# First FFN's down product: two classes as half-array pairs, against four classes as 32-row strips with the weights as the stationary operand

## The reference, cut to what matters

```python
x = x + down(silu(gate(c)) * up(c))     # first FFN, c = per-batch 64x64 condition matrix times x (64 x 64 x 512)
                                        # gate, up: 2048 x 512, down: 512 x 2048, each a cubic spline (Catmull-Rom)
                                        # through 8134 control points laid along the flattened matrix
y = x @ W.T + scale[a] * (x @ A[a].T) @ B[a].T    # adapted layer, a = adapter of the batch (8, rank 16)
x = x + top-2-of-8 experts(y)                     # F = 352, softmax over the two
```

## Time and profile before

| | us |
|---|---|
| runs (median of 3; lowest, highest) | 1277.27; 1273.51, 1279.76 |
| span of the profiled execution (the page gives no other time of it) | 1274.5 |
| PE busy in the span | 1161.4 (91%) |
| PEld / DVE / ACT / POOL busy | 1073.4 / 647.9 / 476.7 / 679.1 |

### The profile page before, as it was taken

The page is one execution under the profiler, slowest core; times in us unless marked ns, Lnnn a source line. Parts: engine busy times, 40 slices in busy tenths (PEclk is TensorE's granted clock), DMA queues, the critical chain, the costliest instruction groups (busy, mean ns, idle before and its releaser), DMA issues. The chain is left out here.

```text
span 1274.5 us, 29820 instructions
## 1 busy us (share of the span) xinstructions
PE 1161.4 (91%) x9814; PEld 1073.4 (84%) x9815; DVE 647.9 (51%) x1223; ACT 476.7 (37%) x1023; POOL 679.1 (53%) x1035
## 2 busy tenths in 40 slices
...
PEclk9769999999999999997999967999999999999998
...
DMA packets 75085, 187.07 MB, mean 147 GB/s; under 512 B 12992, under 2 KB 26056, under 8 KB 70704
## 3 DMA queue, kind: packets, MB, share of 16 engines
...
## 5 line engine op out<-in xcount | busy, mean ns | idle before, releaser
L880 POOL TENSOR_TENSOR in_lo<-inner,in_hi 128x512 fp32r<-128x512 f32 x128 | 168.6, 1317 | 133.4 <-ACT in_hi L1034 133.2
L1577 POOL TENSOR_TENSOR idle<-small 128x1 f32<-128x1 f32 x284 | 93.3, 331 | 196.7 <-DMA out<-result,scatter_at 123.9
L1655 PE MATMUL banks<-slots,zt_hi 128*128 x568 | 190.4, 335 | 4.9 <-DVE zt_lo L1744 2.9
L1657 PE MATMUL banks<-slots,zt_lo 128*128 x568 | 183.8, 324 | 0.0
L1656 PE MATMUL banks<-slots,zt_hi 128*128 x568 | 183.3, 323 | 0.0
L957 PE MATMUL banks<-down_hi,in_hi 64*128 64x320 f32 x1024 | 164.9, 308 | 0.0
L957 PE MATMUL banks<-down_lo,in_hi 64*128 64x320 f32 x1024 | 164.9, 307 | 0.0
L957 PE MATMUL banks<-down_hi,in_lo 64*128 64x320 f32 x1024 | 164.5, 307 | 0.0
L1756 DVE TENSOR_TENSOR hid<-silu_g,banks 128x352 f32<-128x352 f32 x71 | 37.0, 521 | 208.7 <-PE banks L1657 208.7
L1600 POOL DMA_INDIRECT out<-result,scatter_at x71 | 113.7, 1601 | 26.4 <-issue 22.7
L874 POOL TENSOR_TENSOR f_lo<-f_sum,f_hi 128x256 fp32r<-128x256 f32 x128 | 96.3, 769 | 37.8 <-ACT f_hi L1025 34.7
...
## 6 DMA issues: line engine op xcount, KB each, us to landing
...
```

The lines of the kernel that those rows point to most:

```text
L880: nc.gpsimd.tensor_tensor(in_lo[:, cs, :], inner[u % 2][:, :, :], in_hi[:, cs, :].bitcast(F32), ALU.subtract).then_inc(in_done, 1)
L1577: nc.gpsimd.tensor_tensor(idle[:, at:at + 1], small[:, 0:1], small[:, 0:1], ALU.add)
L1655: nc.tensor.matmul(psum[bank][:, 0:FD], zt_hi[:, k, :], w_high, start=(k == 0), stop=False)
L1657: ins = nc.tensor.matmul(psum[bank][:, 0:FD], zt_lo[:, k, :], w_high, start=False, stop=(k == DK - 1))
```

## The change

- **Classes.** The 2048 inner rows and 512 outputs are sorted into 4 classes instead of 2 (32 rows of every chunk and 128 outputs each). A few rows that fall in another class than their output are put right by constants (`c_fix`).
- **Down.** The weights are stationary and the tokens move: 256 columns for both subtiles at once. The four classes take rows 0 to 31, 32 to 63, 64 to 95 and 96 to 127 of the array, each into a bank of its own: three products for a class's outputs (columns 0 to 255 of its bank), two for its powers (columns 256 to 511). All 16 chunks run in two batches of four u, in v = 7 and in v = 1 of the next tile.
- **Sums.** The output is transposed already, so `turn` goes. ACT copies the sums of classes 0 and 3, DVE adds up those of the inner ones (`add_sums`), three steps are split, and `across` has 18 matmuls. One `add` of 1024 elements per tile; x1 is stored transposed, once a tile, into `x1t_dram`.
- **Features.** The condition matrices lie as they are, no longer block-diagonal: each batch's 64 rows make one of a half-array pair. Two groups are one batch (i), i = 3 of a tile comes in v = 0 of its own tile; there are two misc banks, filled and drained together. Moments of both subtiles stand in v = 2.
- **Expert parts.** The three of the down weights come first, and POOL takes their low halves.
- **Layer.** x1 comes transposed into one buffer (two half loads); high and low halves are taken from it directly. PE transposes it back for `out`, ACT copies that (`token_rows`), SP stores it. Expert loads are issued after these, each waiting for the one before.
- **Host side.** Inputs are laid out to fit (tokens of a subtile taken from batches two apart, the residual transposed).
- **Preparation.** The coefficient products are made in two halves (6 matmuls of 256 columns per chunk instead of 3 of 512), with a few small DVE operations for the fix.

The core of the diff (the common indentation is cut):

```diff
-TURN, CLASSES, DPIECES, DWIN = 128, 2, 16, 20
-CLASS_I, CLASS_D = INTER // CLASSES, D // CLASSES
+TURN, CLASSES, DPIECES, DWIN = 89, 4, 16, 20
+CLASS_I, CLASS_D, ROWS = INTER // CLASSES, D // CLASSES, P // CLASSES
+STEPS, STRAYS = CLASSES - 1, 2
...
+def load_x1(sp, t):
+    for h in range(LTILE // TILE):
+        sp.dma_start(x1[:, :, h * TILE:(h + 1) * TILE], x1t_dram[bass.ds(LTILE // TILE * t + h, 1)].rearrange("a p (k n) -> p (a k) n", k=DK)).then_inc(x1_loaded, 16)
...
+PARTS = FC + DK
+DOWN_AT = {1: [(-1, 4), (-1, 5), (-1, 6), (-1, 7)], 7: [(0, 0), (0, 1), (0, 2), (0, 3)]}
+MOMENTS_AT, SUMS_AT, ACROSS_AT, ADD_AT = 2, 2, 3, 4
+FEATURES_AT = {0: [(0, 3)], 4: [(1, 0)], 5: [(1, 1)], 6: [(1, 2)]}
+HIGH_FEATURES_AT = {1: [(0, 3)], 5: [(1, 0)], 6: [(1, 1)], 7: [(1, 2)]}
+PART_AT = {3: [0], 4: [1], 5: [2, 3], 6: [4, 5], 7: [6]}
+F_USES = PAIRS // 2
+USES = 1 + F_USES
...
+def features(t, i):
+    if i == 0:
+        pe.wait_ge(pair_done, t + 1)
+    pe.wait_ge(misc_drained, USES * t + i + 1)
+    for g in (2 * i, 2 * i + 1):
+        at = g % 2 * TILE
         for s in range(SUB):
+            for w, feat in enumerate((feat_hi, feat_lo)):
+                for h in range(2):
+                    rows = slice(h * SEQ, (h + 1) * SEQ)
+                    to = view(misc_bank[h], at + s * SEQ, [[P, 2 - w], [1, SEQ]])
+                    ins = nc.tensor.matmul(to, feat[rows, s, 2 * g:2 * g + 2, :].rearrange("p a n -> p (a n)"), pair[rows, s, 0:2 - w, :],
+                                           start=(w == 0), stop=(w == 1))
+    ins.then_inc(feat_filled, 1)
...
-def down(t, s, u):
+def down(t, u):
     pe.wait_ge(in_done, PAIRS * t + u + 1)
     if u == 0 and not is_int(t, 0):
-        pe.wait_ge(added[s], t)
+        pe.wait_ge(res_added, t)
     for c in (2 * u, 2 * u + 1):
-        for i, (x, w) in enumerate(((in_hi, down_hi), (in_hi, down_lo), (in_lo, down_hi))):
-            for j in range(CLASSES):
-                rows = slice(j * NF, (j + 1) * NF)
-                ins = nc.tensor.matmul(out_bank[s][:, j, 0:NF + CLASS_D], x[rows, c, s * P:(s + 1) * P], w[rows, c, :],
-                                       start=(c == 0 and i == 0), stop=(c == IC - 1 and i == 2))
+        for i, (w, x) in enumerate(((down_hi, in_hi), (down_lo, in_hi), (down_hi, in_lo), (mom_w, in_hi), (mom_w, in_lo))):
+            cols = slice(0, TILE) if i < 3 else slice(TILE, 2 * TILE)
+            for r in range(CLASSES):
+                rows = slice(r * ROWS, (r + 1) * ROWS)
+                ins = nc.tensor.matmul(out_bank[r][:, cols], w[rows, c, :], x[rows, c, :],
+                                       start=(c == 0 and i == 0), stop=(c == IC - 1 and i in (2, 4)), skip_group_check=True)
     if u == PAIRS - 1:
-        ins.then_inc(direct_done[s], 1)
...
+        ins.then_inc(direct_done, 1)
+def across(t):
+    for step in range(STEPS):
+        pe.wait_ge(sums_low, STEPS * t + step + 1)
+        for side, k in ((0, step + 1), (1, STEPS - 1 - step)):
+            item = k - 1 if side == 0 else STEPS + k
+            for i, (w, x) in enumerate(((across_hi, sums_hi), (across_lo, sums_hi), (across_hi, sums_lo))):
+                ins = nc.tensor.matmul(out_bank[k][:, 0:TILE], w[:, item, :], x[:, step, side, :],
+                                       start=False, stop=(i == 2), skip_group_check=True)
+    ins.then_inc(sum_done, 1)
 def body(t):
     for v in range(PAIRS):
         if has_own(t):
             gate_up(t, v)
-        for s, dt, u in DOWN_AT[v]:
-            if has_own(t) if dt == 0 else has_last(t):
-                down(t + dt, s, u)
-        if has_last(t) and v in ACROSS_AT:
-            across(t, t - 1, ACROSS_AT[v])
-        if has_next(t) and v in MOMENTS_AT:
-            moments(t, t + 1, MOMENTS_AT[v])
-        if has_last(t) and v in TURN_AT:
-            turn(t, t - 1, TURN_AT[v])
-        if has_next(t):
-            for g in FEATURES_AT.get(v, []):
-                features(t, t + 1, g)
+        for dt, i in FEATURES_AT.get(v, []):
+            if has(t, dt):
+                features(t + dt, i)
+        for dt, u in DOWN_AT.get(v, []):
+            if has(t, dt):
+                down(t + dt, u)
+        if v == MOMENTS_AT and has_next(t):
+            moments(t + 1)
+        if v == ACROSS_AT and has_last(t):
+            across(t - 1)
...
-def copy_sums(t, s):
-    act.wait_ge(direct_done[s], t + 1)
-    nc.scalar.activation(sums_tok[:, :, :], out_bank[s][:, :, 0:NF], ACT.Copy).then_inc(sums_copied, 1)
-def high_sums(at, s):
-    bank, use = misc_use(at, f"t{s}")
-    act.wait_ge(misc_filled[bank], use + 1)
-    nc.scalar.activation(sums_hi[:, :], misc_bank[bank][:, 0:P], ACT.Copy).then_inc(sums_high, 1)
+def copy_sums(t):
+    act.wait_ge(direct_done, t + 1)
+    nc.scalar.activation(sums[:, 0, :, :], psum[:, OUT:OUT + CLASSES:CLASSES - 1, TILE:], ACT.Copy).then_inc(sums_copied, 1)
+def high_sums(t, step):
+    if step == 0:
+        act.wait_ge(sums_copied, t + 1)
+    else:
+        act.wait_ge(sums_added, (STEPS - 1) * t + step)
+    nc.scalar.activation(sums_hi[:, step, :, :], sums[:, step, :, :], ACT.Copy).then_inc(sums_high, 1)
...
+if v == SUMS_AT and has_last(t):
+    copy_sums(t - 1)
+    high_sums(t - 1, 0)
+if v == MOMENTS_AT + 1 and has_next(t):
+    high_moments(t + 1, 0)
 if has_own(t):
     gate(t, v)
-if v == 0 and has_own(t) and not is_int(t, 0):
-    high_feature(t - 1, PAIRS - 1)
-if has_next(t):
-    for g in FEATURES_AT.get(v - 1, []):
-        high_feature(t, g)
+for dt, i in HIGH_FEATURES_AT.get(v, []):
+    if has(t, dt):
+        high_feature(t + dt, 2 * i)
+        high_feature(t + dt, 2 * i + 1)
+if v == SUMS_AT and has_last(t):
+    high_sums(t - 1, 1)
+    high_sums(t - 1, 2)
+if v == MOMENTS_AT + 1 and has_next(t):
+    high_moments(t + 1, 1)
 if has_own(t):
     high_inner(t, v)
-if has_next(t) and v == 0:
-    pairs(t + 1)
-if has_next(t) and v < SUB:
+if v < SUB and has_next(t):
+    if v == 0:
+        pairs(t + 1)
     high_raw(t + 1, v)
-if has_last(t) and v in COPY_AT:
-    copy_sums(t - 1, COPY_AT[v])
-if has_next(t) and v in MOMENTS_AT:
-    high_moments(t, MOMENTS_AT[v])
-if has_last(t) and v in TURN_AT:
-    high_sums(t, TURN_AT[v])
...
+def add_sums(t, step):
+    if step == 1:
+        dve.wait_ge(sums_copied, t + 1)
+        nc.vector.tensor_tensor(sums[:, 1, :, :], sums[:, 0, :, :], psum[:, OUT + 1:OUT + 3, TILE:], ALU.add).then_inc(sums_added, 1)
+        return
+    dve.wait_ge(sums_added, (STEPS - 1) * t + 1)
+    for side in range(2):
+        ins = nc.vector.tensor_tensor(sums[:, 2, side, :], sums[:, 1, side, :], out_bank[2 - side][:, TILE:], ALU.add)
+    ins.then_inc(sums_added, 1)
+def low_sums(t, step):
+    dve.wait_ge(sums_high, STEPS * t + step + 1)
+    nc.vector.tensor_tensor(sums_lo[:, step, :, :], sums[:, step, :, :], sums_hi[:, step, :, :].bitcast(F32), ALU.subtract).then_inc(sums_low, 1)
+def add(t):
+    dve.wait_ge(res_loaded, 16 * (t + 1))
+    dve.wait_ge(sum_done, t + 1)
+    nc.vector.tensor_tensor(x_res, psum[:, OUT:OUT + CLASSES, 0:TILE], x_res, ALU.add).then_inc(res_added, 1)
...
 for v in range(PAIRS):
+    if v == SUMS_AT and has_last(t):
+        add_sums(t - 1, 1)
+        add_sums(t - 1, 2)
+    if v == MOMENTS_AT + 1 and has_next(t):
+        low_moments(t + 1, 0)
+    if v == ADD_AT and has_last(t):
+        add(t - 1)
     if has_own(t):
         multiply(t, v)
+    if v == MOMENTS_AT + 1 and has_next(t):
+        low_moments(t + 1, 1)
+    if v == SUMS_AT and has_last(t):
+        for step in range(STEPS):
+            low_sums(t - 1, step)
+    for dt, i in FEATURES_AT.get(v, []):
+        if has(t, dt):
+            sum_features(t + dt, i)
+    if v == 0 and has_next(t):
         pairs(t + 1)
+    if v == 1 and has_next(t):
+        for s in range(SUB):
+            low_raw(t + 1, s)
     if has_own(t):
         for i in PART_AT.get(v, []):
...
+def store_out(t):
+    sp.wait_ge(tok_copied, LSUB * (t + 1))
+    sp.dma_start(out_tiles[bass.ds(t, 1)].rearrange("a p s h -> p (a s) h"), x1_tok[:, :, :]).then_inc(out_stored, 16)
+def next_x1(t):
+    sp.wait_ge(x1t_low, LSUB * t)
+    load_x1(sp, t)
 def body(t, n, b, has_next, first):
     if has_next:
-        if not (first and b == 0):
-            sp.wait_ge(filled[X1T[1]], use(t, LSUB - 1) - LSUB // 2 + 1)
-        sp.dma_start(x1[1 - b][:, :, :], layer_tiles[bass.ds(t + 1, 1)].rearrange("a p s h -> p (a s) h")).then_inc(x1_loaded[1 - b], 16)
+        store_out(t + 1)
+        if not (isinstance(t, int) and t == LNT - 2):
+            next_x1(t + 2)
     if first:
+        if b:
+            sp.wait_ge(weights_loaded, LOADS * b)
         load_expert(sp, b, False)
+store_out(0)
+next_x1(1)
 steps(sp, body)
+sp.wait_ge(weights_loaded, LOADS * (SLOTS - 1))
 load_expert(sp, SLOTS - 1, False)
+sp.wait_ge(weights_loaded, LOADS * SLOTS)
...
+def high(t, b, s):
+    if s == 0:
+        act.wait_ge(x1_loaded, 32 * (t + 1))
```

(42 more changed lines are left out.)

437 lines of the change are left out of this document (181 added, 256 removed).

## The result

The changed kernel takes 1354.62 us (median of 4 runs, 1346.86 to 1355.13), the kernel before 1277.07 beside it (4 runs, 1273.51 to 1279.76): a ratio of 1.059, 95% interval 1.056 to 1.062. Forecast were 1257 us and a range of 1233 to 1297. The profiled executions have spans of 1353.4 and 1274.5 us.

| stretch | before | after | difference | forecast |
|---|---|---|---|---|
| start to first gate_up | 76.22 | 70.35 | -5.9 | +1 |
| tile 0 | 29.04 | 30.25 | +1.2 | -2 |
| tiles 1 to 14, each | 30.27 | 33.98 | 14 x 3.71 = +51.9 | -22.4 |
| tile 15 to last residual add | 39.5 | 51.9 | +12.4 | 0 |
| last add to layer's first product | 19.26 | 17.66 | -1.6 | 0 |

What follows compares the result with a forecast made beforehand. PE was taken to bound the first FFN, at 30.15 us a tile. Prologue +1, first tile -2, tiles 1 to 14 -22.4 and layer +3 gave -20.4: span 1254, forecast median 1257 us, range 1233 to 1297.

Steps and rivals of the forecast that it cites:

- Down rounds, 0.122: First FFN on PE: each 256-column round of four strips takes 0.122 us, 80 rounds 9.8 us a tile, a gain of 4.4.
- C: Rival for the down rounds: the four strips don't run abreast; two pairs in turn, 0.236 us a round, give 1394 us; 7%.
- Slots v0 to v5: First FFN tile, slot by slot: v0 2.4 us, v1 0.8 + 4.9, v2 until 3.0, v3 until 6.3, v4 8.7, v5 11.0.
- v6, "DVE its part (0.84) ahead of multiply(6): 3.0": First FFN, slot v6: DVE's weight part, 0.84 us, is queued ahead of multiply(6), so the slot takes 3.0 us.
- Rival B: First FFN: queues on ACT and DVE take all of the gain, 30.1 us a tile, 1279 us; 17%.
- Clock 1.00: First FFN: PE's clock stays at 1.00, full clock, through tiles 1 to 14.
- D: Rival: the clock falls in v4 to v6; halved 3.4 us a tile it costs 1.5 to 3 us, 1279 to 1302; 14%.
- Sum for a tile: First FFN: slots v0 to v7 plus 0.4 for DVE's SBUF operations swinging with POOL, 28.5 us a tile, bounds 27.3 and 30.5.
- Preparation and prologue, +1: Ahead of the first tile: preparation 0, hidden while constants load; prologue +1 us, features batches each behind both reductions of the last.
- Layer, +3: Adapted layer: x1's one buffer makes tile 1's load late, landing at 595 to 598; +3 us (0 to +6).
- Later tiles have 10 us from issue to need: Adapted layer after tile 1: x1 loads, landing after 6.1 us, have 10 us from issue to need.
- Expert loads go out later: 0: Adapted layer: expert loads are issued later and still end long before the experts, 0 us.

Runs made afterwards that it cites:

- e1: The changed kernel with weight parts 3 to 6 moved from v5, v6 and v7 to v7: 1323.22 us, ratio 1.023 to the kernel before.
- e9: The changed kernel with weight part 2 in v4 and POOL taking inner(6) first in v6: 1343.84 us, ratio 1.040 to the kernel before.
- e7: e1 with ten of v7's down rounds issued also in v5 and in v6: 1312.06 us, ratio 1.027 to the kernel before.
- e8: The changed kernel with expert 0's loads in layer tiles 0 and 1, expert 1's in 6 and 7: 1351.06 us, ratio 1.057.

## Why the prediction was wrong

- **Down rounds, 0.122: right** (0.119). C, strips not abreast, is out, and so is its form worked out from the 62 ns a matmul of the Trainium skill ("TensorE: Matmul & The Clock Gate", Back-to-back issue gap), an estimate of 0.248 a round. The Trainium skill's rule in "TensorEngine Tiling (Array Packing)", PSUM Bottleneck, points the right way, and the trace agrees: PE's own work shrank, and the chain that empties the banks set v0, v4 and v5, 2.5 us each with PE busy 1.8 to 2.1. But the large loss was in an operation that touches no PSUM.
- **Slots v0 to v5: right** within 0.2 us, but for v3 (3.90 for 3.4), where the three low halves on DVE, SBUF operations too, kept it busy 2.99 us and not 2.1. That a slot without downs takes 2.4 was read from the last tile and held.
- **v6, "DVE its part (0.84) ahead of multiply(6): 3.0": the step that failed.** v6 took 6.2 on average, the part up to 4.46. The 0.84 was a mean over parts that met POOL for part of their time. On record were 0.4 us a tile for all such swings and a bound of 0.3 to 0.5 an operation. In the kernel before the same operation took 0.51 to 0.53 us in 47 of 64 instances and 1.47 to 1.63 in the 15 that lay under POOL's larger operations: the spread behind the mean was there to read, and with it the row. How much depends on POOL's row, which this change made unbroken: in the short slots v4 and v5 POOL is busy 2.14 and 2.47 of 2.47 us. Shown by e1, by e9 and by the one tile in which the part got through: about 3.2 us a tile. Rival B, queues on ACT and DVE, had the kind of loss and not its size: 30.1 a tile at 17%, where 33.98 came.
- **Clock 1.00: wrong,** as D had it and by more: halved 6.8 to 10.2 us of a tile (9.3 on average) instead of 3.4, v7 7.64 for 6.0, so 1.6 us a tile; e7's two tiles show what the same v7 takes at full clock. Much of the +12.4 in tile 15 and the end is the same by the trace, which has half clock for 27.3 of these 51.9 us, but nothing was run on that. D was priced as if the clock fell only in the slots that have no downs; it fell at their end and lay on the batch behind them, where every round counts.
- **Sum for a tile:** 28.5 + 3.2 (v6) + 1.6 (v7) + 0.5 (v3) = 33.8; the other slots are 0.6 over the layout, of which the allowance held 0.4. Measured 33.98.
- **Preparation and prologue, +1: wrong in sign,** -5.9. The moments of tile 0 start at 56.4 instead of 61.5. Nothing was run on why.
- **Layer, +3: one wait right, the rest missed.** The wait at layer tile 1 is 5.3 us. "Later tiles have 10 us from issue to need" took a landing of 6 us; beside experts' loads it took 10 to 14, and x1's one buffer passes that on: 9.3 us of wait in two tiles, -10.2 us when the loads are spaced (e8). These waits are 14.6 of the +18.3; the rest was not taken apart. "Expert loads go out later: 0" looked only at when they end.
